# Gelu stage of a Flamingo block: ring of eight slices for the high and low parts, second product four slices behind, and a new order in a batch

## The reference, cut to what matters

```
inter = gelu(x2 @ fi_w + fi_b)                    # 256 -> 1024
h     = layernorm(inter @ fo_w + fo_b + x2) * fo_g + fo_be
y     = x + tanh(g_xattn) * h
hn    = (normalised y, rms scaled);  logits = hn @ gate_w.T   # 8 experts, the top 2 are taken
```

## Time and profile before

| what | value |
|---|---|
| median of 3 runs | 1977.41 us (1977.0 to 1981.69) |
| profiled execution, first to last instruction | 1978.4 us |
| mean granted TensorE clock | 0.959 |
| PE busy | 1788.8 us, 90% of the span |
| DVE busy | 1404.5 us, 71% |
| ACT busy | 1221.4 us, 62% |
| POOL busy | 1217.9 us, 62% |

### The profile page before, as it was taken

One profiled execution on the slowest core, in us unless ns is written; L12 is line 12 of the kernel. 1 busy time (PEld: TensorE's weight loads), 2 busy tenths in 40 slices (PEclk: granted clock), 3 DMA queues, 4 the chain that ended last, 5 costly groups with the idle time before them and its releaser, 6 DMA issues. The chain is left out here.

```text
span 1978.4 us, 36354 instructions
## 1 busy us (share of the span) xinstructions
PE 1788.8 (90%) x12326; PEld 1325.6 (67%) x12326; DVE 1404.5 (71%) x2786; ACT 1221.4 (62%) x2305; POOL 1217.9 (62%) x1117
## 2 busy tenths in 40 slices
PE   0799999999999999999985999923999999999995
PEld 0455555555555555555545888923999999999995
DVE  5378788787887878888833877844667667766762
ACT  0167777676776767777753554413777777777773
POOL 6635657565665744556336466551787778878775
PEclk9999999999999999999987999956999999999998
DMA  3665554665655565555412122126667667666762
GB/s 93 120 136 118 123 133 106 118 139 123 135 114 125 106 128 130 124 126 108 83 60 73 49 102 76 70 80 219 216 212 231 215 210 226 220 222 208 230 216 33
DMA packets 125198, 274.80 MB, mean 139 GB/s; under 512 B 15803, under 2 KB 57915, under 8 KB 124629
## 3 DMA queue, kind: packets, MB, share of 16 engines
q1 hardware_dynamic: 110708, 253.77, 47.0%
q0 software_dynamic: 14304, 18.72, 4.7%
HBM read 196.50 MB, written 75.92 MB: 138 GB/s over the span
## 5 line engine op out<-in xcount | busy, mean ns | idle before, releaser
L706 DVE TENSOR_REDUCE nz<-ps 128x1 f32<-128x512 f32 x1024 | 650.8, 684 | 182.9 <-PE ps L845 180.9
L620 ACT ACTIVATE spare<-ps 128x512 f32<-128x512 f32 x1024 | 571.3, 601 | 267.1 <-PE ps L855 263.0
L1743 POOL TENSOR_TENSOR u_lo<-u_f,u_hi 128x256 fp32r<-128x256 f32 x273 | 376.8, 1397 | 142.4 <-ACT u_hi L1777 142.3
L1849 PE MATMUL ps_e<-x_hi,we_hi 128*128 128x256 f32 x1092 | 312.9, 287 | 4.9 <-DVE we_lo L1663 4.9
L1849 PE MATMUL ps_e<-x_lo,we_hi 128*128 128x256 f32 x1092 | 305.7, 280 | 0.0
L1849 PE MATMUL ps_e<-x_hi,we_lo 128*128 128x256 f32 x1092 | 305.7, 280 | 0.0
L855 PEld LDWEIGHTS ps<-qst,kst 52*128 52x128 f32 x1024 | 102.0, 184 | 277.3 <-ACT spare L620 189.8
L867 PE MATMUL ps<-spare,vaug 128*32 128x512 f32 x2048 | 274.9, 609 | 0.0
L845 PE MATMUL ps<-kst,qst 50*128 50x512 f32 x1024 | 264.1, 442 | 10.9 <-issue 10.1
L855 PE MATMUL ps<-qst,kst 52*128 52x512 f32 x1024 | 269.2, 501 | 3.7 <-ACT spare L620 3.3
L1703 DVE TENSOR_TENSOR u_f<-ps_e,silu 128x256 f32<-128x256 f32 x273 | 115.1, 422 | 180.9 <-ACT silu L1808 176.3
(11 more groups left out here) (224 smaller groups left out, 3620.0 us busy)
## 6 DMA issues: line engine op xcount, KB each, us to landing
we_raw<-in_experts_w SPq DMA_DIRECT2D x117, 896.0 KB, 4.9
parts_kept<-parts SPq DMA_DIRECT2D x64, 512.0 KB, 3.9
kst<-parts_kept SPq DMA_DIRECT2D x192, 128.0 KB, 4.3
qst<-parts_kept SPq DMA_DIRECT2D x192, 128.0 KB, 5.3
x_raw<-xs SPq DMA_DIRECT2D x39, 259.0 KB, 2.8
maxima<-nsplit SPq DMA_DIRECT2D x64, 128.0 KB, 3.5
x<-sum_tok SPq DMA_DIRECT2D x16, 512.0 KB, 2.7
x_tok<-x SPq DMA_DIRECT2D x16, 512.0 KB, 4.1
```

What stands on the lines that cost most here:

```text
L620: act.activation(probs[:, e % 8], ps[:, score_bank(e, par)], ACT.Exp, scale=SCALE).then_inc(exp_made, 1)
L706: dve.tensor_reduce(nz[:, g % 2, place:place + 1], ps[:, max_bank(m, par)], AX.X, ALU.max, negate=True).then_inc(max_made, 1)
L1743: pool.tensor_tensor(u_lo[:, it], u_f[:, q % UPS], u_hi[:, it].bitcast(F32), ALU.subtract).then_inc(ulo_made, 1)
L1849: ins = pe.matmul(ps[:, q % UPS, c * GR:(c + 1) * GR], left, right, start=m == 0, stop=m == len(terms) - 1)
```

## The change

- `in_hi` and `in_lo` become rings of eight slices (a whole batch); `gelu_out` stays a ring of four. ScalarE's high part waits for the second product of the same slice of the batch before, instead of the slice four back.
- The second product runs four steps behind (`FO_LAG`): slices 4 to 7 of batch i-1 fall into steps 0 to 3 of period i.
- TensorE: the logits move from step 3 to step 2, `turn_in` from steps 4 and 6 to steps 3 and 5, there behind the rank matmuls.
- ScalarE: `high_in` moves with `turn_in`, to steps 3 and 5.
- VectorE: its low slice comes first in every step instead of last; `low_hn` moves from step 2 to 1, `layer_sum` from 2 to 3, in front of `layer_moments`; `low_in` moves from steps 4 and 6 to 3 and 5; `gated_sum` from 4 to 5; `hidden` from 6 to 7.
- GpSimd: `s_root_of` moves from step 3, ahead of its slices 3 and 4, to step 5, behind them; `y_root_of` from 6 to 7.

```diff
+FO_LAG = 4
@@ gelu_phase
-    in_hi = sb("gelu_hi", [P, 4, S], F32R)
-    in_lo = sb("gelu_lo", [P, 4, S], F32R)
+    in_hi = sb("gelu_hi", [P, KF, S], F32R)
+    in_lo = sb("gelu_lo", [P, KF, S], F32R)
+    def fo_bank(qt):
+        return ps[:, FO + qt, 0:D]
@@ GpSimd
-                    if first and s == 3:
-                        s_root_of(i - 1)
                     if gelu and s in POOL_LO:
                         pool.wait_ge(in_hi_made, i * KF + s + 1)
-                        pool.tensor_tensor(in_lo[:, s % 4], gelu_out[:, s % 4],
-                                           in_hi[:, s % 4].bitcast(F32), ALU.subtract) \
+                        pool.tensor_tensor(in_lo[:, s], gelu_out[:, s % 4],
+                                           in_hi[:, s].bitcast(F32), ALU.subtract) \
                             .then_inc(lo_pool, 1)
-                    if first and s == 6:
+                    if first and s == 5:
+                        s_root_of(i - 1)
+                    if first and s == 7:
                         y_root_of(i - 1)
@@ ScalarE
-                        if n >= 0:
-                            if m == KF - 1:
-                                act.wait_ge(fo_done, QT * (n // KF + 1))
+                        if i:
+                            if s == KF - 1:
+                                act.wait_ge(fo_done, QT * i)
                             else:
-                                act.wait_ge(fo_mm, (KF - 1) * (n // KF) + m + 1)
-                        act.activation(in_hi[:, s % 4], gelu_out[:, s % 4], ACT.Copy) \
+                                act.wait_ge(fo_mm, (KF - 1) * (i - 1) + s + 1)
+                        act.activation(in_hi[:, s], gelu_out[:, s % 4], ACT.Copy) \
                             .then_inc(in_hi_made, 1)
...
-                    if s in (4, 6) and following:
-                        high_in(i + 1, (s - 4) // 2)
+                    if s in (3, 5) and following:
+                        high_in(i + 1, (s - 3) // 2)
@@ VectorE, period
                 for s in range(KF):
-                    if s == 2:
-                        if second:
-                            for mt in range(KD):
-                                low_hn(i - 2, mt)
+                    if gelu and s in DVE_LO:
+                        low_slice(i, s)
+                    if s == 1 and second:
+                        for mt in range(KD):
+                            low_hn(i - 2, mt)
+                    if s == 3:
                         if first:
                             layer_sum(i - 1)
-                    if s == 3 and first:
-                        layer_moments(i - 1)
-                    if s == 4:
-                        if second:
-                            begun[0] = route_to_picks(i - 2)
-                        if first:
-                            gated_sum(i - 1)
+                            layer_moments(i - 1)
                         if following:
                             low_in(i + 1, 0)
-                    if s == 5 and first:
-                        sum_moments(i - 1)
-                    if s == 6:
-                        if second:
-                            route_to_slots(i - 2, begun[0])
+                    if s == 4 and second:
+                        begun[0] = route_to_picks(i - 2)
+                    if s == 5:
                         if following:
                             low_in(i + 1, 1)
                         if first:
-                            hidden(i - 1)
-                    if gelu and s in DVE_LO:
-                        low_slice(i, s)
+                            gated_sum(i - 1)
+                            sum_moments(i - 1)
+                    if s == 6 and second:
+                        route_to_slots(i - 2, begun[0])
+                    if s == 7 and first:
+                        hidden(i - 1)
@@ TensorE, period
-                    if s < 3 and first:
-                        second_product(i - 1, KF - 3 + s)
-                    if s >= 3 and gelu:
-                        second_product(i, s - 3)
+                    if s < FO_LAG and first:
+                        second_product(i - 1, KF - FO_LAG + s)
+                    if s >= FO_LAG and gelu:
+                        second_product(i, s - FO_LAG)
...
-                    if s == 3 and second:
+                    if s == 2 and second:
                         b = i - 2
...
-                    if s == 4 and following:
+                    if s == 3 and following:
                         turn_in(i + 1, 0)
...
-                    if s == 6 and following:
+                    if s == 5 and following:
                         turn_in(i + 1, 1)
```

More of the change, by code:

```diff
@@ L1214, in low_slice @@
                 dve.wait_ge(in_hi_made, i * KF + s + 1)
-                dve.tensor_tensor(in_lo[:, s % 4], gelu_out[:, s % 4],
-                                  in_hi[:, s % 4].bitcast(F32), ALU.subtract).then_inc(lo_dve, 1)
+                dve.tensor_tensor(in_lo[:, s], gelu_out[:, s % 4],
+                                  in_hi[:, s].bitcast(F32), ALU.subtract).then_inc(lo_dve, 1)
             def layer_sum(b):
@@ L1223, in layer_sum @@
                     dve.wait_ge(fo_done, b * QT + qt + 1)
-                    dve.tensor_tensor(s_tok[:, qt], ps[:, FO + qt, 0:D], x2_tok[:, b % 3, qt],
+                    dve.tensor_tensor(s_tok[:, qt], fo_bank(qt), x2_tok[:, b % 3, qt],
                                       ALU.add).then_inc(sum_made, 1)
@@ L1435, in second_product @@
                     c = slice(qt * P, (qt + 1) * P)
-                    terms = split_products(in_hi[:, mt % 4, c], in_lo[:, mt % 4, c], fo_hi[:, mt],
+                    terms = split_products(in_hi[:, mt, c], in_lo[:, mt, c], fo_hi[:, mt],
                                            fo_lo[:, mt])
                     for n, (left, right) in enumerate(terms):
-                        ins = pe.matmul(ps[:, FO + qt, 0:D], left, right, start=mt == 0 and n == 0,
+                        ins = pe.matmul(fo_bank(qt), left, right,
+                                        start=mt == 0 and n == 0,
                                         stop=mt == KF - 1 and n == len(terms) - 1)
```

## The result

The changed kernel takes 1996.37 us (median of 5 runs, 1990.51 to 1997.21), the kernel before 1977.41 us (5 runs, 1975.54 to 1981.69): 1.0080 times as long, 95% interval 1.0057 to 1.0103. It is slower, by more than this measurement's 0.3%. The profiled execution took 1992.03 us.

The account below looks back on a forecast made before the run. It took TensorE to bound the kernel. Picks waits 18.3 + clock 6.2 + logits 1.6 - removed waits 13.6 = +12.5 us on the profiled 1978.4 us gives 1990.9, with the median 1.0 us under: 1990 us, range 1975 to 2002.

Parts of the forecast that it names:

- Removed, 13.6 us on offer: TensorE's waits on s_tok, gelu_lo and the input's low half, and three slow-clock stretches, would go: 13.6 us from batch 2.
- Waits on picks, 18.3 us: TensorE would wait for VectorE's picks before the rank matmuls: 3.3 us in batches 3 to 7, 1.8 in batch 2.
- The unheld part: Wait on picks with VectorE undisturbed: its 7.2 us of work against TensorE's 6.1, so 1.1 us in batches 2 to 7.
- The hold: GpSimd's slices 3 and 4 would delay VectorE's layer_moments, lengthening the picks wait from 1.1 to 3.3 us in batches 3 to 7.
- t=0: The end on TensorE of sp(i-1,7), the previous batch's last second-product slice; forecast at picks + 21.1 us.
- If slice 3's Gelu comes later: Case in which GpSimd's slices partly miss VectorE's layer_moments; the picks wait was then counted as 2.8 us.
- VectorE held by GpSimd: VectorE operations between two SBUF tiles would wait for GpSimd's current operation; without this the sum would be 11.5 us less.
- Rival A: VectorE isn't held: picks waits of 1.1 us in six batches, no slow stretch, 1971.5 us, faster; chance 0.12.
- The clock, 6.2 us: Picks waits would bring TensorE's low clock in about four of batches 3 to 7, 1.55 us each: 6.2 us.
- The logits waiting, 1.6 us: TensorE's logits, now two slices after turn_hn, would wait for hn_lo: 0.4 us in each of four batches.
- The end, 0 (-1.4 to +2.6): After the last first product: same TensorE work, batch 6's logits now ahead of sp(7,7); taken as 0, from -1.4 to +2.6 us.
- where late signals held it before, nothing: At the end, logits ahead of sp(7,7) would delay layer_sum(7) at most 2.6 us, or nothing if late signals already held it.

Follow-up runs that it names:

- e8: The kernel before with the 24 logits matmuls in four parts, at steps 3 and 4, instead of one piece: 1978.64 us, ratio 0.9999 to before.
- e10: The kernel before with the scatter's eight issues split, four at step 7 and four behind base in the next period: 1972.47 us.
- e11: The kernel before with both the logits in four parts and the scatter's issues split in four and four: 1969.94 us, ratio 0.9970 to before.
- e7: The changed kernel with GpSimd's slice 4 on 64 of its 512 columns in all batches but the first: 1985.43 us.
- e2: The changed kernel with the logits at TensorE's step 3, behind sp(i-1,7), instead of step 2: 1991.97 us.
- e12: The changed kernel with the scatter's eight issues split in four and four: 1993.16 us, ratio 1.0075 to before.
- e5: The changed kernel with the rank matmuls at step 6 instead of 5 and the 24 logits matmuls in four parts of six: 1981.93 us.

## Why the prediction was right, and where it was off

It said 1990 us, in 1975 to 2002, slower with 0.77; measured were 1996.37. The sum was +12.5 us on the stage, the traces differ by +16.1. By its steps:

*Removed, 13.6 us on offer.* Right in what goes: the s_tok waits and the steady g_lo waits left the list. But it read TensorE as the bound and these waits as its loss. e8 shows that the round of before (29.7 us) is set by VectorE, the scatter's issues and late signals: without any low stretch the stage is as long. So the clock stretches in it cost nothing that could be won alone. With the signals on time (e10) TensorE bounds the steady batches again, at 29.0 us; with its clock whole as well (e11) they are at 28.7, and it waits.

*Waits on picks, 18.3 us.* Right in place and number (six times), too large in size: 12.0 us. The unheld part was forecast at 1.1 us and is about 0.9 (e7). The hold was forecast at 2.2 us for batches 3 to 7, with slices 3 and 4 ending at t=4.5 and 5.9. In the batch shown base ended at t=1.0 instead of 3.1. It was not early itself: it ended 23.8 us behind the picks before it, near the 24.2 of the prediction. But t=0 came 22.8 us behind these picks instead of 21.1, since a low stretch that the prediction had elsewhere lies between. Slice 4 waited for its Gelu and ran from t=3.3 to 4.8. Slice 3 met BATCH_NORM_STATS2, which isn't held, so one gain was held once, 1.0 us. The nearest case that the prediction mentions ("If slice 3's Gelu comes later") it counted too high, at 2.8.

*VectorE held by GpSimd.* Shown: L1243's like, L1247, is held, and so is s_var (up to 3.91 us, e2). Rival A (not held, 1971.5 us) is out. The Trainium skill (SBUF — State Buffer, Terms) calls the port pair that VectorE and GpSimd share exclusive and held for the whole instruction, the loser fully blocked; the trace agrees (in e12 a low slice of 0.7 us took 5.76 under residual and base). It adds nothing to the sum above.

*The clock, 6.2 us.* Undersized, and put in the wrong place. Seven low stretches came, not four, and six of them begin 3.0 to 4.8 us behind the start of the logits. Ahead of four of these TensorE had not been idle for 15 us (in batch 2 it had idled 1.4 us shortly before the logits, and in batch 7 it idled 1.0 us within them); only the one at 1252.4 lies behind a wait for picks. The batch of 30.75 us is 27.20 + 1.90 of wait + 1.65 of clock, so seven cost 11.5 us, less three in before. e5, e8 and e11 show what the stretches behind the logits need: 24 matmuls of 8 columns in one piece; in four pieces no such stretch comes. The piece alone isn't enough, since in before only three of six are followed by one. The prediction took the idle time ahead of them in the earlier trace rows for the cause; but in before's own trace the longest of the four waits for s_tok (1.23 us, before 1175.5) has logits behind it at 1176.98 and no low stretch.

*The logits waiting, 1.6 us.* No wait in the list names hn_lo. There are 1.0 us ahead of the last logits matmul of batch 7, put down to issue; hn_lo had been complete since 1267.35, so their cause stays open. And there are 1.4 us for hn_tok in batch 2, which were not forecast: 2.4 us.

*The end, 0 (-1.4 to +2.6).* It cost 3.1 us, just outside the bounds. All of it lies ahead of sp(7,7): sp(7,6) ended at 1294.84 and sp(7,7) started at 1297.91, and between them stand 0.4 us of idle time (hn_lo had ended at 1295.15, the logits started at 1295.21) and 2.7 us of logits, both of which in before come behind sp(7,7). From the end of sp(7,7) to x_raw it is 73.98 us before and 73.95 after. (From the start of batch 6's logits to x_raw it is 73.6 before and 78.3 after, but these 4.7 us hold sp(7,7) itself, which in before stands ahead of that mark; the expectations of e2 and e12 measure in this way.) Timelines of TensorE, GpSimd and VectorE in after:

```profile
1299.30 0.28 PE L1440 MATMUL ps_g<-fo_hi,gelu_lo 128*128 128x256 f32 x1
1310.21 0.21 PE L1489 MATMUL ps_g<-picks,before 128*128 128x32 bf16 x1 [10.63 <-DVE picks L1321]
```

```profile
1300.07 0.96 POOL L1094 DMA_INDIRECT xs<-hn_tok,slot_now  x1 [0.30 <-issue]
```

```profile
1302.88 1.42 DVE L1228 TENSOR_TENSOR s_tok<-ps_g,x_tok 128x256 f32<-128x256 f32 x4 [7.73 <-remote]
```

The product ended at 1299.57; VectorE, idle since 1295.15, started layer_sum at 1302.88. In before it was held too: the product ended at 1287.43, the second half of layer_sum started at 1290.40. So the step "where late signals held it before, nothing" failed: the time of the logits that now lie ahead of sp(7,7) did not vanish in the lateness, it came on top of it, since the signals are late behind the later product too. e12 (the issues split) takes the lateness away and 4.5 us with it.

In sum, with both sides by the traces: 12.0 + 11.5 + 2.4 + 0.6 (gelu_out) + 3.1 - 13.6 = 16.0 us against 16.1 measured. So the terms are all there, though the 1.65 us of a stretch comes from one batch. That 12.5 came near 16.1 is partly luck: the waits on picks were 6.3 us too large in the forecast, the clock 5.3 and the end 3.1 too small.

By the prediction's own signs: the mean wait on picks, 2.0 us, lies between the 3 that it expected and the 1 that would have shown it wrong. In the batch shown slice 3 started at base's end, one L1247 took over 1 us (in all batches but the last), and the batches took 30.7 to 32.3 us, near its 31 to 32.5. The low clock came behind the logits and not behind the rank matmuls.

## What to carry to other kernels

Before counting an engine's waits as its loss, follow the round: if an edit that makes the busiest engine faster turns its busy time into idle one for one (e8: -2.9 and +3.1 us), another round of engines sets the pace. When a wait goes from one place to the next (picks, turn_in, hn_lo), stop moving the waiting instruction and shorten what stands ahead of it. When GpSimd's operation moves, look up which VectorE operation will run under it: under BATCH_NORM_STATS2 or a read out of PSUM it costs nothing, under one between SBUF tiles it costs what is left of it.

## What the runs showed of the hardware

TensorE's signals can arrive late while GpSimd issues indirect DMAs. In after the matmuls that end at 1298.05, 1298.51, 1298.86, 1299.22 and 1299.57 have their semaphore events at 1302.70 to 1302.91, in one burst; the last of eight issues ended at 1301.03. In before such bursts begin 1.1 to 1.6 us behind the last issue, in five batches. With four issues at a time the signals of the second product's last slice came within 0.02 us of their matmuls in e10, and within 0.11 us in e11 and e12 as far as their events are recorded, so it takes a row of issues longer than four, or something that starts behind the fourth; which one, and by what path a signal waits, no run here shows. In the views it is seen only as idle time put down to "remote".

TensorE's granted clock can fall behind a run of narrow matmuls with no idle time near it: 24 of 8 columns, back to back for 2.6 us, were followed by 3.4 us at 1.2 GHz in the six batches of after (in four of them with no idle time for 15 us ahead), by a stretch at 1.2 GHz in five of six in e10 and in three of six in before, and in none of e5, e8 and e11, where they stand in four parts. What decides it where they stand in one, no run here shows.
